# Turning the normed FFN rows by transposing DMAs in a fused long-convolution and FFN kernel

## The reference, cut to what matters

```python
# x, ctx: (8, 128, 256); 16 heads of 8 channels, L = 256
def xattn(k, v, q, ssm_kernel, D, head_dim):
    kv = einsum('bhil,bhjl->bijhl', k, v)          # k = v = ctx: products of channels of one head
    y = causal_convolution(kv, ssm_kernel[h])      # along l, by FFT in the reference
    out = y + kv * D[h]
    return einsum('bijhl,bhil->bjhl', out, q)      # q = layernorm(x)
x = x + xattn(ctx, ctx, layernorm(x), ssm_kernel, D, 8)
def ffn(x):                                        # 256 -> 704 -> 256, int weights minus 128, scaled
    return qlinear(silu(qlinear(x, Wg, sg)) * qlinear(x, Wu, su), Wd, sd)
x = x + ffn(layernorm(x))
```

## Time and profile before

| what | value |
|---|---|
| median of three runs | 78.2 us (78.01 to 78.25) |
| span of the profiled execution, first to last instruction | 76.7 us |
| around the span, median less span | 1.5 us |
| busy: TensorE matmul, VectorE, GpSimd, ScalarE | 70.7, 63.9, 54.6, 46.7 us |
| mean granted TensorE clock | 0.990 |

### The profile page before, as it was taken

How to read it: one execution, slowest core, us unless ns; L and a number is a source line. 1 busy time by engine, 2 the same in 40 slices (tenths; PEclk the granted TensorE clock), 3 DMA queues, 4 the chain that set the end, 5 groups by cost and what they waited for, 6 DMA issues and landing times.

```text
span 76.7 us, 1495 instructions
## 1 busy us (share of the span) xinstructions
PE 70.7 (92%) x469; PEld 57.8 (75%) x469; DVE 63.9 (83%) x191; ACT 46.7 (61%) x115; POOL 54.6 (71%) x73
## 2 busy tenths in 40 slices
PE   4999988879999999999999999999999999999920
PEld 3767735568798777787888797988897989899810
DVE  0088399969999999899999999999999993786760
ACT  0601483275859587976868468746767798766400
POOL 5004798799889599299899949459627899939230
PEclk9999999999999999999999999999999999999995
DMA  0498999999997000000000000000000222200404
GB/s 5 132 256 279 386 344 295 285 384 397 386 353 220 13 0 0 0 0 4 4 9 0 0 0 0 0 0 0 0 9 4 68 68 68 68 9 0 137 0 137
DMA packets 7304, 8.29 MB, mean 108 GB/s; under 512 B 992, under 2 KB 6400, under 8 KB 7296
## 3 DMA queue, kind: packets, MB, share of 16 engines
q1 hardware_dynamic: 6912, 8.00, 31.7%
q10 hardware_dynamic: 384, 0.19, 0.8%
HBM read 7.12 MB, written 1.07 MB: 107 GB/s over the span
## 4 chain that ended last, share of the span: by engine, by line
PE 58%; DMA 15%; DVE 14%; SPq 3%; ACT 3%; issue 2%; DVEq 0%; ACTq 0%
PE conv L1010 18%; PE turn L957 8%; PE down L1029 8%; DMA k_ext<-ctx_ext 8%; DMA toeplitz<-taps 7%; PE conv L977 6%; PE conv L988 6%; PE conv L986 6%; DVE hidden L733 3%; DVE terms L718 2%; PE turn L939 2%; DVE terms L721 2%; PE turn L1029 2%; SPq L310 2%; ACT gate_act L508 1%
## 5 line engine op out<-in xcount | busy, mean ns | idle before, releaser
L1010 PE MATMUL conv<-f_parts,wgu 128*128 128x256 f16 x176 | 21.6, 273 | 0.3
L1010 PEld LDWEIGHTS conv<-f_parts,wgu 128*128 128x128 f16 x176 | 16.7, 98 | 3.5 <-DVE hidden L733 0.8
L376 POOL TENSOR_TENSOR products<-k_ext 128x512 f32<-128x512 f32 (+1 forms) x16 | 18.0, 1144 | 0.6 <-DMA k_ext<-ctx_ext 0.6
L508 ACT ACTIVATE gate_act<-conv,sg_sb 128x256 f32<-128x256 f32 (+1 forms) x24 | 11.2, 471 | 4.6 <-PE conv L1010 4.0
L258 POOL TENSOR_TENSOR h_lo<-hidden,h_hi 128x256 fp32r<-128x256 f32 x18 | 12.9, 729 | 1.4 <-ACT h_hi L513 1.3
L733 DVE SCALAR_TENSOR_TENSOR hidden<-conv,su_sb,gate_act 128x256 f32<-128x256 f32 (+1 forms) x24 | 11.3, 479 | 3.1 <-ACT gate_act L508 2.7
L977 PE MATMUL conv<-products,toeplitz 128*128 128x288 f32 x32 | 11.2, 434 | 0.3 <-DVE terms L725 0.3
L365 POOL TENSOR_TENSOR rstd_f<-variance_f,minus_half 128x1 f32<-128x1 f32 x8 | 5.5, 683 | 7.9 <-DVE variance_f L694 7.9
L718 DVE TENSOR_TENSOR terms<-conv,q_ext 128x512 f32<-128x512 f32 x16 | 10.8, 678 | 0.0
L986 PE MATMUL conv<-products,toeplitz 128*128 128x288 f32 x32 | 10.8, 422 | 0.0
L988 PE MATMUL conv<-products,toeplitz 128*128 128x288 f32 x32 | 10.4, 406 | 0.0
(11 more groups left out here) (64 smaller groups left out, 119.8 us busy)
## 6 DMA issues: line engine op xcount, KB each, us to landing
k_ext<-ctx_ext SPq DMA_DIRECT2D x3, 384.0 KB, 6.1
toeplitz<-taps_pad SPq DMA_DIRECT2D x2, 512.0 KB, 7.9
out<-x_sb SPq DMA_DIRECT2D x8, 128.0 KB, 1.7
toeplitz<-taps SPq DMA_DIRECT2D x3, 256.0 KB, 5.3
wg_int<-wg_t SPq DMA_DIRECT2D x1, 704.0 KB, 8.2
wu_int<-wu_t SPq DMA_DIRECT2D x1, 704.0 KB, 9.5
wd_int<-wd_t SPq DMA_DIRECT2D x1, 640.0 KB, 8.6
x_sb<-x SPq DMA_DIRECT2D x1, 512.0 KB, 7.0
```

The source lines that it names most:

```text
L376: nc.gpsimd.tensor_tensor(view(products[:, n:n + 1], first * MADE + GROUP, [[MADE, halves], [GROUP, 4], [1, GROUP]]), view(k, 0, [[EXT * B ...
L508: nc.scalar.activation(gate_act[up_lanes(t), i % 2, t, :], gate_of(i, t), ACT.Silu, scale=sg_sb[gate_lanes(t), t:t + 1]).then_inc(gate_act ...
L1010: done = nc.tensor.matmul(bank_of(i, t)[:, n, :], wgu[:, c, column:column + P], f_parts[:, i % 2, part, c, :], start=(c == 0 and part == 0 ...
```

## The change

The two TensorE transposes of each tile (`turn_f`) are gone. The split is now made ahead of the turn, in SBUF: `high_f` copies `f_rows` to f16 in a new buffer `f_split`, `low_f` subtracts that from `f_rows` into `f_split`, and SyncE issues one transposing DMA per tile, 128 rows by 512 f16 numbers (128 KB), from `f_split` to `f_parts`. `gates(i, 0)` waits for the two DMAs of its block. `norm_f` now waits for `low_f` of the tile two before, and `high_f` for the DMA of the tile two before. The skip weights come as the first 16 columns of k's buffer and, for the taps, in an unused column of the taps, in place of two DMAs of their own on ScalarE's list. `fill` is 14 matmuls in place of 17. The lists of all five engines have a new order.

```diff
-        k_ext = sb("k_ext", [P, H, HALVES, EXT * B])
+        k_skip = sb("k_skip", [P, H + H * HALVES * EXT * B])
+        skip_all = k_skip[:, 0:H]
+        k_ext = k_skip[:, H:].rearrange("p (h c n) -> p h c n", h=H, c=HALVES)
+        f_split = sb("f_split", [P, 2, 2, L], F16)
@@ sync
+            def turn_f(t):
+                wait(sp, f_high, t + 1)
+                wait(sp, f_low, t + 1)
+                wait(sp, gate_up_done, CHUNKS * (t // BLOCK_TILES - 1))
+                sp.dma_start_transpose(parts_of(t), f_split[:, t % 2].rearrange("p a l -> p (a l)")).then_inc(
+                    f_loaded[t], 16)
+            turn_f(0) ... turn_f(5)
+            store(0, 0)
+            turn_f(6)
+            turn_f(7)
+            store(0, 1)
@@ scalar
             def norm_f(t):
                 wait(act, f_shift, t + 1)
+                wait(act, f_low, t - 1)
             def high_f(t):
-                wait(act, f_turned, t + 1)
-                nc.scalar.activation(parts_of(t, 0), turned..., ACT.Copy).then_inc(f_high, 1)
+                wait(act, f_normed, t + 1)
+                if t >= 2:
+                    act.wait_ge(f_loaded[t - 2], 16)
+                nc.scalar.activation(f_split[:, t % 2, 0], f_rows[:, t % 2, :], ACT.Copy).then_inc(f_high, 1)
-            act.dma_start(skip_all[:, :], skip...).then_inc(skip_loaded, 16)
             act.dma_start(x_sb[:, 0, :], x[0:P, :]).then_inc(x_loaded[0], 16)
             act.dma_start(taps_sb[:, :], taps).then_inc(taps_loaded, 16)
-            act.dma_start(skip_sb[:, :], skip).then_inc(taps_loaded, 16)
@@ scalar, order: norm_q(2), evict_q(2) and wrap(1) move ahead of the wait for k of heads 8 to 11
+            norm_q(2)
+            evict_q(2)
+            wrap(1)
             act.wait_ge(k_loaded[4], 16)
@@ vector
             def low_f(t):
                 wait(dve, f_high, t + 1)
-                dve.tensor_tensor(parts_of(t, 1), turned..., parts_of(t, 0), ALU.subtract).then_inc(f_ready, 1)
+                dve.tensor_tensor(f_split[:, t % 2, 1], f_rows[:, t % 2, :], f_split[:, t % 2, 0],
+                                  ALU.subtract).then_inc(f_low, 1)
@@ vector, order: the start
+            dve.wait_ge(x_loaded[0], 16)
+            stats_of_q(0)
             dve.wait_ge(k_loaded[0], 16)
             all_products(0, 0, 1)
@@ vector, order: multiply_terms(2) and (3) and add_sum(0) now ahead of this wait
+            dve.wait_ge(x_loaded[3], 16)
+            stats_of_q(4)
@@ vector, order: around the last multiply_terms
-            multiply_terms(15)
-            hidden_units(1, 4)
-            low_f(5)
+            low_f(5)
+            scale_out(0, 0)
+            multiply_terms(14)
+            scale_out(0, 1)
+            hidden_units(1, 3)
+            hidden_units(1, 4)
+            multiply_terms(15)
+            add_sum(6)
             hidden_units(1, 5)
+            merge_back(dve, 7)
             stats_of_f(6)
-            merge_back(dve, 7)
+            merge_last(dve, 7)
@@ tensor
-            def turn_f(t, free, count): ...
             def gates(i, t):
                 if t == 0:
-                    wait(pe, f_ready, BLOCK_TILES * (i + 1))
+                    pe.wait_ge(f_loaded[BLOCK_TILES * i], 16)
+                    pe.wait_ge(f_loaded[BLOCK_TILES * i + 1], 16)
-            fill(turn[:, 0:2 * P], 17)
+            fill(turn[:, 0:2 * P], 14)
@@ tensor, the new order from the last sum_terms to the last gates
+            sum_terms(7, x1_ready, 7)
             downs(1, 3)
             gates(2, 2)
+            downs(1, 4)
             gates(2, 3)
+            gates(2, 4)
             downs(1, 5)
             gates(2, 5)
             downs(2, 0) ... downs(2, 5)
             gates(3, 0) ... gates(3, 5)
             downs(3, 0) ...
```

More of the change, by code:

```diff
@@ L309, in load_k @@
             def load_k(first, last, done):
-                sp.dma_start(k_ext[:, first:last], ctx_ext[:, first:last]).then_inc(done, 16)
+                row = HALVES * EXT * B
+                columns = slice(H + first * row if first else 0, H + last * row)
+                sp.dma_start(k_skip[:, columns], ctx_skip[:, columns]).then_inc(done, 16)
             def load_x(first, last, done):
@@ L824, in _ @@
-            shift_of_f(1)
+            merge_back(dve, 2)
+            variance_of_f(1)
+            multiply_terms(6)
+            low_f(0)
+            shift_of_f(1)
+            shift_of_q(5)
+            multiply_terms(7)
+            low_f(1)
+            stats_of_q(6)
+            multiply_terms(8)
+            moments_of_q(6)
+            multiply_terms(9)
+            add_sum(2)
+            stats_of_q(7)
+            merge_back(dve, 3)
+            moments_of_q(7)
+            variance_of_q(6)
@@ L825, in _ @@
+            merge_last(dve, 3)
             stats_of_f(2)
-            low_f(0)
-            multiply_terms(8)
-            low_f(1)
+            variance_of_q(7)
+            merge_back(dve, 4)
             moments_of_f(2)
-            multiply_terms(9)
-            merge_back(dve, 3)
+            shift_of_q(6)
+            add_sum(3)
+            variance_of_f(2)
             dve.wait_ge(scales_loaded, 3 * 16)
             hidden_units(0, 0)
-            variance_of_f(2)
-            merge_last(dve, 3)
@@ L853, in _ @@
-            add_sum(4)
+            merge_last(dve, 4)
+            shift_of_f(2)
+            stats_of_f(3)
+            hidden_units(0, 1)
+            moments_of_f(3)
+            shift_of_q(7)
+            variance_of_f(3)
+            multiply_terms(10)
+            shift_of_f(3)
+            low_f(2)
+            multiply_terms(11)
+            add_sum(4)
+            hidden_units(0, 2)
+            merge_back(dve, 5)
+            low_f(3)
+            merge_last(dve, 5)
+            hidden_units(0, 3)
@@ L854, in _ @@
             multiply_terms(12)
-            low_f(2)
             stats_of_f(4)
-            merge_back(dve, 5)
+            hidden_units(0, 4)
             moments_of_f(4)
-            hidden_units(0, 4)
-            low_f(3)
+            add_sum(5)
+            variance_of_f(4)
+            multiply_terms(13)
+            stats_of_f(5)
+            shift_of_f(4)
             hidden_units(0, 5)
-            multiply_terms(13)
-            variance_of_f(4)
-            merge_last(dve, 5)
+            moments_of_f(5)
@@ L933, in turn_q @@
                 done.then_inc(q_turned, 1)
-            def turn_f(t, free, count):
-                wait(pe, f_normed, t + 1)
-                wait(pe, free, count)
-                for c in range(HALVES):
-                    done = nc.tensor.transpose(turned[:, c * P:(c + 1) * P], f_rows[:, t % 2, c * P:(c + 1) * P],
-                                               ident[:, :])
-                done.then_inc(f_turned, 1)
             def sum_terms(t, free, count):
@@ L1110, in _ @@
-            gates(1, 3)
             downs(0, 4)
             downs(0, 5)
-            sum_terms(6, f_ready, 5)
+            gates(1, 3)
+            sum_terms(6, x1_ready, 6)
+            gates(1, 4)
             convolve(15)
-            gates(1, 4)
             gates(1, 5)
-            turn_f(5, x1_ready, 7)
             downs(1, 0)
```

360 lines of the change are left out of this document (158 added, 202 removed).

## The result

The changed kernel takes 86.89 us (median of four runs, 86.74 to 87.05) against 78.16 (78.01 to 78.25, four runs beside it): a ratio of 1.1125, 95% interval 1.1102 to 1.1148. It is 8.7 us slower. The prediction said 77.6 us and a range from 76.4 to 79.5.

The account below looks back on a forecast made before the run. VectorE was taken to decide when `sum_terms(7)` starts, with fixed TensorE work behind it. Starting 0.97 us earlier, plus 0.4 of DMA wait, gave -0.57: 78.2 to 77.6 us, range 76.4 to 79.5.

Parts of the forecast that it names:

- T: End of the last `multiply_terms` on VectorE: predicted at 54.51 us, against 54.75 in the old trace.
- TensorE was the bound: Rival, chance 0.10: all 1.76 us of removed transposes come off and the DMA hides, giving 76.4 us.
- Idle time of VectorE: Before the last `multiply_terms`: 0.75 us of idle removed at 15 to 20 us, 0.38 at 20 to 60.
- The 0.75 at 16.28: VectorE's idle wait for x's tiles 4 to 7, all taken off because the new list puts other work first.
- the fourth of T: Six `low_f` with two SBUF inputs before the last `multiply_terms` ends: up to 0.17 us each, 0.5 added.
- From T to `sum_terms(7)`: VectorE's work between the last `multiply_terms` and that sum: 2.41 us against 3.14, so the sum starts at 56.92.
- Behind `sum_terms(7)`: Fixed list of TensorE work to the end, unchanged: two transpose pairs (0.44 us) out, four `downs` matmuls (0.47) in.
- The DMA: Transposing DMA before `gates(3, 0)`: landing taken as 3.1 us, bounds 1.7 and 7.5, so a wait of 0.4 us.
- The slack of 2.7: Time in us from tile 7's parts being ready (61.62) to TensorE reaching `gates(3, 0)` (64.36).
- The start: Rival, chance 0.08: with 14 zero matmuls TensorE pauses, its clock rises later, 0.5 to 1.5 us lost, about 78.4.
- The 1.5 us around the span: Time outside the traced span: taken as the only difference between the trace's 76.7 us and the median's 78.2.
- Skip weights: Two small DMAs off ScalarE's list: zero gain, since with full DMA engines what is issued sooner lands no sooner.

Follow-up runs that it names:

- experiment 3: Kernel before, with only the second input of `low_f` read from SBUF (`f_rows`, not turned) in place of PSUM: 79.83 us, ratio 1.025.
- experiment 8: Kernel before, with GpSimd's products of channels replaced by a memset of constants: 78.03 us, ratio 1.002.
- experiment 10: Kernel before, with only the new loads: skip weights inside k's buffer and the taps, two small DMAs gone: 78.09 us, ratio 1.0027.
- experiment 1: Changed kernel, with `low_f` replaced by a statistics instruction of the same width with one SBUF input: 83.86 us, ratio 1.079.
- experiment 9: Changed kernel, with `low_f` as a one-input statistics instruction and GpSimd's products of channels as a memset: 79.79 us, ratio 1.025.
- experiment 7: Changed kernel, with GpSimd's products of channels replaced by a memset of constants: 81.25 us, ratio 1.042 from a single execution.
- experiment 12: Changed kernel's lists, loads and 14 zero matmuls, but the turn on TensorE as before, in one placing: 91.83 us, ratio 1.175.
- experiment 4: Kernel before in its own lists and loads, with the split in SBUF and the transposing DMAs: 92.46 us, ratio 1.187.
- experiment 11: Changed kernel, with the turn of q tile 0 back behind the second convolution in TensorE's list: 87.75 us, ratio 1.127.

## Why the prediction was wrong

The four corners, in us: old lists with TensorE's turn 78.0, old lists with the DMA 92.5, new lists with TensorE's turn (in one placing) 91.8, new lists with the DMA 86.9. Neither half is good alone. The new lists were needed to hide the DMA, and both halves brought two SBUF inputs of VectorE together with GpSimd's reads.

The prediction put `sum_terms(7)` at 56.92 and the span at 76.1; they came out at 64.29 and 84.9. Of the error of some 8.7 us, T is 6.7 (54.51 against 61.19), the way from T to the sum 0.7, and what lies behind the sum 1.3 (0.4 of waiting predicted, 1.7 of other kinds measured). So two terms of T failed, one mis-sized and one put at nothing without a reason, and a smaller one behind the sum.

- **What bounds the kernel.** Right: VectorE decides when `sum_terms(7)` can start; TensorE waits 0.95 us there for `merge_last`. The rival "TensorE was the bound" did not come true; no run takes TensorE's transposes out alone, so what their 1.76 us would give by themselves was not measured.
- **Idle time of VectorE.** The number was near, by luck: 0.75 + 0.38 = 1.13 us predicted, 1.42 measured. The 0.75 at 16.28 belonged to the one execution that was traced. The old lists show none of it in the traces of experiments 3, 8 and 10 (5.00 us busy of 5.00 from 15 to 20), so no new order could take it off the median. From 20 to 60 VectorE idles 0.37 in the changed kernel, but 0.49 in experiment 1 and 0.72 in experiment 9, where its instructions are shorter: at least part of what looks like idle time saved was filled with waiting inside instructions.
- **The step that failed first** is the fourth of T: "So up to 0.17 each, for the six `low_f` before T 1.0 us; none if GpSimd is the one that is held up. I take the middle, 0.5." Measured: 4.10 - 0.41 = 3.7 us for the six. The bound was the mean of four h_tail subtractions, half a tile high. One of them, 0.67 us at 48.48, met only the last 0.4 us of a product that GpSimd had begun at 47.58; one, at 66.75, took 0.84 behind most of an `h_lo`; the other two took 0.42, one of them beside a root of GpSimd and one beside nothing. A mean of few meetings is no bound on one meeting. The bound was in the trace: one whole instruction of the other engine, 1.28 us for GpSimd's merge, and then the waiting instruction itself. Six times 1.28 would have been 7.7 us, so a kernel several us slower belonged in the range.
- **The term put at nothing.** The prediction moved instructions between lists at their old lengths, without saying so. For `direct`, the merges and the products that was wrong by 4.1 us before T, more than `low_f` itself. The old lists kept `direct` and `merge_back` out of GpSimd's products; for example, in the old trace GpSimd ran only its small roots from 12.6 to 14.5 us, and three diagonal additions of 0.34 us lie there. The new lists have two GpSimd products from 12.52 to 15.09 and a diagonal addition of 1.18 us at 14.06. Experiments 7 and 12 show both sides of this.
- **The page quoted.** The Trainium skill (SBUF — State Buffer, "Who interferes with whom") says the exclusion holds for a whole instruction. For GpSimd's wide instructions the trace agrees: 1.48 us on a 0.41 us instruction. For its roots, one column wide, it does not: no VectorE instruction was longer for beginning inside one. The prediction named the rule and then capped it with 0.17 us from a row, which the rule does not allow.
- **From T to `sum_terms(7)`.** Predicted 2.41, measured 3.10: `merge_back(7)` 1.03 and `merge_last(7)` 0.87 in place of 0.67 and 0.69, the same cause.
- **Behind `sum_terms(7)`.** The prediction called this a fixed list of TensorE work. It grew by 1.7 us, in every trace with the new lists and the DMA. TensorE idles 0.7 of it; VectorE's `h_tail` at 67.67 took 1.01 us and its two `h_lo` 0.69 on the mean. How much is collisions and how much the new order was not taken apart.
- **The DMA.** Landing 2.4 us against 3.1 taken, within the bounds; the wait before `gates(3, 0)` did not come, since everything on TensorE's side was later. The slack of 2.7 was right in kind: at a landing of 2.4 it would have been hidden in the predicted order too. In the old lists (experiment 4) all four blocks waited, up to 3.6 us: 2.3 us are the DMA from the start of its issue to its landing, and in blocks 1 and 2 the issue began 1.2 us after TensorE had reached its wait, since the split comes ahead of it. The Trainium skill (VectorE: DVE Perf Modes, "The three transpose paths") gives 1.309 us for a 128 by 128 turn; the measured 2.4 for four such blocks speaks against adding them up, to an estimate of 5.2.
- **The start.** That rival did not come true, but its sign was a poor one. With 14 zero matmuls the first convolution's steps start 0.79 and 0.59 us apart from 4.84 on, faster than the 1.09 of the earlier trace rows. With the 17 of the kernel before they are 0.56 and 0.49 from 4.47 on in the trace of experiment 10, and with 14 again 1.09 in that of experiment 11. So the 1.09 varies between executions, and no run here shows that it hangs on the number of zeros. Nor does the granted clock read 1.00 there, as I had it: that trace holds no value of it before 6.89 us, just when the steps shorten, and the view prints 1.00 where it has none. In the other three traces its first value, 1.00, is at 4.13, 3.75 and 6.01 us, and the steps are short from about there on.
- **The 1.5 us around the span.** In the other executions of the kernel before the time is 1.7 to 1.9 us above the span, with spans of 75.5 to 76.9 around a median of 76.1. The traced one, 76.7, was thus a few tenths of a us longer than most.
- **Skip weights.** Zero, shown by experiment 10.
- **What stays open.** The 1.7 us behind `sum_terms(7)`, which are also most of the 1.8 between experiments 9 and 8. GpSimd's merges and `h_lo` were not taken away separately. Keeping the f32 rows in PSUM, so that `low_f` has one SBUF input, was not tried.

No version here beats the kernel before, and the experiments point to none: with every GpSimd product and every two-input `low_f` out, the changed order still stands at 79.8, against 78.0.

## What to carry to other kernels

Before moving an instruction between PSUM and SBUF or along a list, mark those VectorE instructions that read two SBUF tensors and those GpSimd instructions that read SBUF over many columns; each meeting can cost one whole instruction of the other side, whatever the width of the one that waits. The waiting shows as longer instructions and not as idle time, so compare mean lengths by group before and after. When both lists are tuned by hand, the old order may be what kept the meetings apart, so that instructions that a diff only moves do not keep their lengths. One trace is one execution: look whether a pause that you mean to remove is there in a second one. A DMA in place of a TensorE step needs slack for the work ahead of it and for the way from the start of its issue to its landing, here 2.4 us; where TensorE waits for it, the clock that falls afterwards costs more on top, here 1.0 to 1.3 us behind waits of 2.8 to 3.6.

## What the runs showed of the hardware

- A VectorE subtraction of one column (128 by 1) took 145 ns alone and up to 1225 ns against GpSimd's 1.28 us products; the 128 by 256 one 409 to 1486 ns. GpSimd lost less: its products grew from 1284 to 1363 ns on the mean, h_lo from 729 to 812, its busy time by 2.5 us against VectorE's 8.8.
- In the traces of the two kernels GpSimd's one-column roots lengthened no VectorE instruction with two SBUF inputs: an `h_tail` subtraction kept its 0.42 us inside a root of 0.55.
- With 0.52 us memsets in place of GpSimd's products, diagonal additions kept 339 ns.
- A transposing DMA of 128 by 512 f16 in SBUF: 1.19 us of issue on SyncE and landing 2.4 us after the start of the issue, in all eight cases within 0.1 us. The store of the same 128 KB lands in 1.7, of which 0.33 are its issue. So the transposing one takes 0.7 us longer by its issue alone: behind the end of the issue it is 1.2 us against 1.4. The Trainium skill (Advanced Engine Details and Errata, "X-Bar Transpose (TRN2)") has transposing DMAs as fast as regular ones; for the way behind the issue the trace agrees.
- After TensorE had waited 2.8 to 3.6 us, 16 f16 matmuls of 256 columns took 2.9 to 3.3 us and not 1.9; with zero matmuls in most of the wait and 0.94 and 1.33 us of pause left, 1.9. The pause of 2.35 us at 6.9 us was followed by full speed in the changed kernel, as was one of 2.00 in experiment 4, and one of 2.45 us in experiment 9 by a granted clock of 0.57 from 10 to 14 us: pauses of this length went either way.
